# The first projection chain of a two-layer cross-attention kernel in two groups, and the last out-projections inside the last unit

## The reference

```
layer 0:  x = x + selfattention(LN(x))
          x = x + crossattention(LN(x), LN(context))        16 heads of 8 channels
          h = LN(x); x = h's residual x + top-2 of 8 experts (gelu MLP of width 512)
layer 1:  x = x + crossattention'(LN(x), context), its four weight matrices made ternary
each attention: softmax(q k^T / sqrt(8)) v, then out-projection with bias
```

## Time and profile before

| what | value |
|---|---|
| runs of the kernel before | 583.17, 574.94, 576.57 us |
| median | 576.57 us |
| the profiled execution | 574.07 us, of which the span of instructions is 572.3 us |
| PE, DVE, ACT, POOL busy | 514.1, 390.0, 334.4, 221.3 us |
| TensorE clock granted, mean of the span | 0.962 of full |

### The profile page before, as it was taken

The page is one execution under the profiler, slowest core; times in us unless marked ns, Lnnn a source line. Parts: engine busy times, 40 slices in busy tenths (PEclk is TensorE's granted clock), DMA queues, the critical chain, the costliest instruction groups (busy, mean ns, idle before and its releaser), DMA issues.

```text
span 572.3 us, 16262 instructions
## 1 busy us (share of the span) xinstructions
PE 514.1 (90%) x6648; PEld 386.4 (68%) x6648; DVE 390.0 (68%) x976; ACT 334.4 (58%) x527; POOL 221.3 (39%) x217
## 2 busy tenths in 40 slices
PE   3599748889999999999989999999998999999996
PEld 2588515466767767676767998877666676766774
DVE  5666378788887888787741434887867777786730
ACT  1166223557676777776576444376666667675573
POOL 3659744475777768423160200031404033140000
PEclk9799677899999999999999999999999999999998
DMA  5110552634354554555638401006354835535200
GB/s 160 48 55 3 143 122 50 169 89 132 95 139 112 143 145 101 137 120 143 182 73 223 141 2 31 2 1 154 72 150 113 201 92 140 144 85 121 56 4 9
DMA packets 37869, 58.69 MB, mean 103 GB/s; under 512 B 17956, under 2 KB 21404, under 8 KB 37796
## 3 DMA queue, kind: packets, MB, share of 16 engines
q1 hardware_dynamic: 37476, 57.60, 39.8%
q10 hardware_dynamic: 320, 0.06, 0.1%
HBM read 17.81 MB, written 0.23 MB: 32 GB/s over the span
## 4 chain that ended last, share of the span: by engine, by line
PE 68%; DVE 17%; POOL 4%; DMA 3%; issue 3%; ACT 2%; SPq 2%; DVEq 0%; ACTq 0%; POOLq 0%
PE PO L1386 14%; PE SM L1371 14%; DVE mxp L883 11%; PE ST L1343 10%; PE MI L1292 8%; PE ST L1564 4%; PE ST L1554 4%; PE MI L1282 3%; PE MI L1271 2%; POOL cxs L518 2%; PE MI L1318 2%; DMA xT<-in_ctxT 1%; ACT pts L671 1%; PE SM L1477 1%; SPq L393 1%
## 5 line engine op out<-in xcount | busy, mean ns | idle before, releaser
L883 DVE TENSOR_REDUCE mxp<-SM 112x1 f32<-112x500 f32 x374 | 241.0, 673 | 74.4 <-PE SM L1371 73.2
L671 ACT ACTIVATE pts<-ST 128x896 f32<-128x896 f32 x192 | 171.7, 913 | 31.3 <-PE ST L1343 30.8
L1371 PE MATMUL SM<-kst,qst 96*112 96x500 bf16 x374 | 142.2, 399 | 13.0 <-DVE mxp L883 9.0
L527 POOL TENSOR_TENSOR kr<-kf,ksplit 128x500 f32<-128x500 f32 x48 | 55.1, 1150 | 172.4 <-ACT ksplit L636 172.4
L1343 PEld LDWEIGHTS ST<-qst,kst 98*128 98x128 bf16 x1536 | 95.8, 100 | 29.5 <-issue 4.7
L1343 PE MATMUL ST<-qst,kst 98*128 98x112 bf16 x1536 | 106.9, 213 | 2.6 <-DMA qst<-mrow 2.6
L1386 PE MATMUL PO<-pts,vaug 125*32 125x112 f32 x3072 | 97.3, 263 | 2.3 <-ACT pts L671 1.9
L1371 PEld LDWEIGHTS SM<-kst,qst 96*112 96x112 bf16 x374 | 45.6, 129 | 61.5 <-DVE mxp L883 45.0
L1386 PEld LDWEIGHTS PO<-pts,vaug 125*32 125x32 f32 x3072 | 69.3, 109 | 14.8 <-ACT pts L671 5.7
L518 POOL TENSOR_SCALAR cxs<-cxs,cmv,crstd 125x128 f32<-125x128 f32 x84 | 67.4, 819 | 0.0
L532 POOL TENSOR_TENSOR ksplit<-kr,ksplit 128x500 bf16<-128x500 f32 x48 | 54.4, 1135 | 16.9 <-DVE ksplit L878 16.9
(11 more groups left out here) (156 smaller groups left out, 539.8 us busy)
## 6 DMA issues: line engine op xcount, KB each, us to landing
kst<-ksplit SPq DMA_DIRECT2D x192, 187.5 KB, 3.6
cxs<-in_ctx SPq DMA_DIRECT2D x8, 750.0 KB
xT<-in_ctxT SPq DMA_DIRECT2D x8, 750.0 KB, 6.5
qst<-qall SPq DMA_DIRECT2D x56, 21.0 KB, 1.9
watt<-in_watt SPq DMA_DIRECT2D x1, 768.0 KB, 5.5
cxs<-in_w1T SPq DMA_DIRECT2D x3, 256.0 KB, 5.7
cxs<-in_w2T SPq DMA_DIRECT2D x3, 256.0 KB, 6.3
pts<-in_w1T SPq DMA_DIRECT2D x3, 256.0 KB, 5.4
```

Source lines behind the costliest of these rows:

```text
L527: nc.gpsimd.tensor_tensor(kr[:, c], kf[:, c], ksplit[n.par][:, 0, c], ALU.subtract).then_inc(kr_done, 1)
L671: nc.scalar.activation(PT[:, k % PTB], ST[:, k % 2, :, 0:4 * PC], ACT.Exp, scale=SCALE).then_inc(exp_done, 1)
L883: nc.vector.tensor_reduce(mxp[:, j // 3, j % 3:j % 3 + 1], tile_bank(j, banks), AX.X, ALU.max).then_inc(sm_red, 1)
L1371: mm(tile_bank(j, banks), qst[n.par][0:SROWS, j // 3], kst[n.par][0:SROWS, j // 3, at:at + THIRD], start=True, stop=True).then_inc(sm_full, 1)
```

## The change

The four tiles' first chain becomes two groups (`PARTS`): tile 0 alone, and tiles 1 to 3.

- Tile 0's chain runs in steps 8 to 11 of self-attention, whose scores bank SM[0] is free by then: out-projection and statistics in step 8 (POOL's power ahead of the one for unit 2's context), normalise and transpose in 9, gain and query projection in 10, split in 11. Its six DMAs follow unit 0's restack; the load of unit 3's context moves behind them.
- After self-attention PE projects unit 1's keys and two thirds of unit 0's values, and the start tiles begin, 21 in place of 18. Both halves of `place_q` stand before them.
- The chain of tiles 1 to 3 stands among the start tiles: out-projection after tile 2 on PE, addition and statistics after tile 3 on DVE, and so on to the split after tiles 14 to 16. Statistics of unit 3's context stand at tile 12 and in steps 3 and 4 of the first window, which has 27 tiles in place of 30.
- POOL computes `token_rstd(2)` between `k_rest` and `k_third_part` of unit 1.
- In every out-projection the bias matmul comes first and the wait stands behind it.
- At the end: the out-projection of tiles 0 and 1 of layer 1 moves from window 5 to step 3 of window 7, tile 2's goes to its step 10, and only tile 3's is left for the end, with one store each.
- The second half of layer 1's query chain moves by a few steps, and its DMAs from SP's window 1 to window 2.

```diff
-START_TILES = 18
+START_TILES = 21
-FIRST_TILES = spread_tiles(TILES - START_TILES, (3, 3, 3, 3, 2, 2, 3, 3, 2, 2, 2, 2))
+FIRST_TILES = spread_tiles(TILES - START_TILES, (3, 3, 3, 3, 2, 2, 2, 2, 2, 2, 2, 1))
-LN5_AT, Q2_AT = (1, 3), (1, 9)
+LN5_AT, Q2_AT = (0, 10), (1, 10)
+START_OUT, START_ADD, START_NORM, START_LN, START_Q, START_SPLIT = 2, 3, 7, 9, 13, (14, 15, 16)
...
+PARTS = (range(0, 1), range(1, TT), range(0, HT), range(HT, TT), range(0, HT), range(HT, TT))
+OUT_PARTS = (range(0, 1), range(1, TT), range(0, HT), range(HT, TT), range(0, HT), range(HT, HT + 1), range(HT + 1, TT))
+OUT_MISC = (0, 2, 4, 5)
...
             load_ctx(Unit(0, None, 2))
-            load_ctx(Unit(0, None, 3))
             restack(u0, 0)
             restack(u0, 1)
             load_qall(0)
+            load_ctx(Unit(0, None, 3))
             place(u1, 0)
             restack(u1, 0)
+            load_qall(1)
...
                 if i == 8:
+                    token_rstd(1)
                     ctx_rstd(u0 + 2)
...
-            token_rstd(1)
+            k_parts(u1, None, lambda: token_rstd(2))
             ctx_normalise(u0 + 2, (2,))
-            k_parts(u1, None)
-            ctx_rstd(u0 + 3)
...
+                if i == 8:
+                    add_projection(0)
+                    token_stats(1)
+                if i == 9:
+                    token_normalise(1)
+                if i == 10:
+                    token_gain(1)
+                if i == 11:
+                    split_q(0)
...
             place_q(first, 0)
+            place_q(first, 1)
             for j in range(START_TILES):
                 reduce_tile(first, j, banks=4)
+                if j == START_ADD:
+                    add_projection(1)
+                    token_stats(2)
+                if j == START_NORM:
+                    token_normalise(2)
+                if j == START_LN:
+                    token_gain(2)
+                if j in START_SPLIT:
+                    split_q(1, (START_SPLIT.index(j),))
-                if j in (1, 4, 7):
-                    k_second_part(first + 1, j // 3)
+                if j in (1, 5, 12):
+                    k_second_part(first + 1, (1, 5, 12).index(j))
+                if j == TILES // 2:
+                    ctx_stats(u0 + 3, range(6))
...
-                    mm(tile, attnT[:, TP * t:TP * (t + 1)], watt[:, layer, 3], start=True, stop=False)
-                    last = mm(tile, ones_row[:], rows[0:1, D * layer:D * (layer + 1)], start=False, stop=True)
+                    mm(tile, ones_row[:], rows[0:1, D * layer:D * (layer + 1)], start=True, stop=False)
+                    if i == 0:
+                        pe.wait_ge(*done)
+                    last = mm(tile, attnT[:, TP * t:TP * (t + 1)], watt[:, layer, 3], start=False, stop=True)
...
-                    if n.s == 1 and (n.c, k) == OUT_AT:
-                        prev = project_out(3, (ont_evac, B + B // 2), prev)
+                    if n.s == 1 and (n.c, k) == (7, 3):
+                        prev = project_out(4, (ont_evac, B + B // 2), prev)
+                    if n.s == 1 and (n.c, k) == (7, 10):
+                        prev = project_out(5, (ont_evac, B + B - 2), prev)
...
             for j in range(START_TILES):
                 max_tile(u0, j, banks=4)
-                if j in (1, 4, 7):
-                    prev = project_v(u0, j // 3, prev)
-                if j in (10, 13, 16):
-                    prev = transpose_ctx(u0 + 2, (10, 13, 16).index(j), prev)
+                if j == 0:
+                    prev = project_v(u0, 2, prev)
+                if j == START_OUT:
+                    project_out(1, (sa_att, B))
+                if j == START_LN - 1:
+                    prev = transpose_tokens(2, prev)
+                if j == START_Q - 1:
+                    prev = project_q(1, prev)
+                if j in (10, 14, 17):
+                    prev = transpose_ctx(u0 + 2, (10, 14, 17).index(j), prev)
```

More of the change, by code:

```diff
@@ L437, in window @@
                     restack(nxt, 1)
+                if n.s == 1 and n.c == 2:
+                    load_qall(3)
                 if n.s == 0 and (n + 4).exists():
@@ L445, in window @@
                     load_xT(xT_unit)
-                if n.s == 1 and n.c == 1:
-                    load_qall(2)
                 if n.s == 0 and n.c in (3, 4):
@@ L474, in _ @@
             rows_out = out.rearrange("(t p) d -> p t d", p=TP)
-            for h in range(2):
-                sp.wait_ge(x_added, 4 + h)
-                sp.dma_start(rows_out[:, HT * h:HT * (h + 1)], xt[:, HT * h:HT * (h + 1)]).then_inc(stored, 16)
-            sp.wait_ge(stored, 32)
+            for n in range(4, 7):
+                sp.wait_ge(x_added, n + 1)
+                ts = OUT_PARTS[n]
+                sp.dma_start(rows_out[:, ts[0]:ts[-1] + 1], xt[:, ts[0]:ts[-1] + 1]).then_inc(stored, 16)
+            sp.wait_ge(stored, 48)
         @block.gpsimd
@@ L558, in window @@
                     k_parts(k_unit, None)
+                if n.first():
+                    ctx_rstd(n + 3)
                 if n.s == 0 and (n + 3).exists():
@@ L729, in evac_piece @@
                     evac_xT(n, (third,))
-                else:
+                if kind == "k":
                     evac_k(n, third)
@@ L824, in token_gain @@
                     dve.wait_ge(ld_vec, 16)
-                cols = slice(TP * token_tiles(n)[0], TP * (token_tiles(n)[-1] + 1))
-                src = SM[:, 0, 0:N] if n < 2 else MI[:, 0:HN]
+                cols = token_cols(token_tiles(n))
+                src = (SM[:, 0] if n < 2 else MI)[:, 0:cols.stop - cols.start]
                 nc.vector.tensor_scalar(hT[:, cols], src, ln_vec(X_LN[n], 0), ln_vec(X_LN[n], 1),
@@ L830, in split_q @@
             def split_q(n, parts=range(3)):
-                c = slice(0, N) if n == 0 else slice(HN * (n - 1), HN * n)
-                src, layer = (SM[:, 0, 0:N], 1) if n == 0 else (MI[:, 0:HN], 2)
+                c = token_cols(Q_TILES[n])
+                src, layer = (SM[:, 0] if n == 0 else MI)[:, 0:c.stop - c.start], n // 2 + 1
                 if 0 in parts:
@@ L1063, in window @@
                         copy_gates(0)
+                    if n.s == 1 and (n.c, k) == (0, 4):
+                        token_stats(6)
                     if n.s == 1 and (n.c, k) == (0, 9):
[L1065 removed]
+                        token_normalise(6)
                     if n.s == 1 and (n.c, k) == (0, 11):
[L1067 to L1069 removed]
+                        token_gain(6)
                     if n.s == 1 and (n.c, k) in SPLIT2_AT:
[L1071 to L1073 removed]
+                        split_q(3, (SPLIT2_AT.index((n.c, k)),))
+                    if n.s == 1 and (n.c, k) == (7, 5):
+                        add_projection(4)
+                    if n.s == 1 and (n.c, k) == (7, 11):
+                        add_projection(5)
+                    if n.first() and k == 3:
+                        ctx_stats(n + 3, range(6, NCH))
+                    if n.first() and k == 4:
+                        dve.wait_ge(cstat_ready, (n + 3).count(1, 1))
+                        ctx_aggregate(n + 3)
                     if ln_unit is not None:
@@ L1465, in piece @@
                     return transpose_ctx(n, third, prev)
-                return project_k(n, third, prev)
+                if kind == "k":
+                    return project_k(n, third, prev)
+                if kind == "out":
+                    pe.wait_ge(ld_rows, 48)
+                    pe.wait_ge(sa_sub, B)
+                    project_out(0, (sa_att, 2))
+                if kind == "ln":
+                    transpose_tokens(1, (x_added, 1))
+                if kind == "q":
+                    project_q(0, (hT_ready, 2))
+                return prev
             for i in range(SA_STEPS):
```

146 lines of the change are left out of this document (66 added, 80 removed).

## The result

The changed kernel takes 582.23 us in the median of 20 runs (577.62 to 590.4), the kernel before 577.96 us in 20 runs beside them (573.65 to 583.3). The ratio is 1.0077, 95% interval 1.0048 to 1.0105: slower by 0.8%, about 4.4 us (2.8 to 6.1), and so within 2%. I had forecast 577.5 us, in the range 572.5 to 583. The time is inside it, near its upper end, and the sign is right; but the three parts of the sum are all off: the start one way, the middle and the end the other.

A forecast was written before the change was run, and what follows sets the result against it. PE was taken to bound the whole span, DVE the start tiles. Start +3.4, middle 0 and end -1.2 gave +2.2 us on a base of 575.3: 577.5 us, range 572.5 to 583.

The forecast's parts named there:

- step 1: Self-attention: tile 0's addition and statistics on DVE delay unit 2's power and the restack by 1.8 us, bounds 0 to 3.
- step 2: Start: after restacks and `qall` transfers the first max tile comes at 81.5 instead of 86.14, a gain of 4.6 us.
- step 3: First tile to window 1: DVE's work, with unit 3's context and the chain of tiles 1 to 3, sums to 45.2 us.
- rival C: Start tiles: casts of keys and split slow down beside POOL; if two suffer, +4 us, 581.5 us; chance 0.05.
- step 4: First tile to window 1: DVE idles 7.0 us, 4.0 in the start tiles and 3.0 in the first window.
- step 5: Window 1 starts at 134.2 instead of 130.8, 3.4 us later, bounds 129.7 to 138.7.
- The middle: Layer 1's second query chain moves by some steps; nothing there waited before, so 0 us, bounds -0.5 to +0.5.
- The end: Last out-projections and store: end 2.0 us nearer, window 5 gains 1.6, window 7 loses 2.4; net 1.2 us gained.
- A: Start: the added DVE work slides into its idle time, if idle stays below 4.8 us; 573.5 us, chance 0.28.
- B: First window: unit 1's restack comes late and PE stalls 3 us for `kst` in step 1; 580.5 us, chance 0.15.
- D: Start: `qall` issues or self-attention slip 3 us more, first tile at 84.5 or later; +5, 580.5 us; chance 0.05.
- The signs: Expected trace marks: `place_q` waiting, DVE over 85% busy in start tiles, scores at 104 to 107, store about 2 us nearer.

The follow-up runs named there:

- e1: The changed kernel with layer 1's second query chain and the end put back as before, so only the start changed: 588.02 us, ratio 1.0175 to the kernel before.
- e5: The changed kernel with the chain of tiles 1 to 3 ahead of the first tile, casts of K and values placed as before: 568.83 us, ratio 0.9836.
- e7: The changed kernel with both the chain of tiles 1 to 3 and unit 3's context statistics ahead of the first tile: 567.51 us, ratio 0.9817.
- e10: The changed kernel with unit 1's second cast of K after tile 2 in place of tile 5: 580.34 us, ratio 1.0067.
- e9: The changed kernel with nine unread matmuls on PE, six ahead of the first tile, three ahead of the tokens' transposes: 581.8 us, ratio 1.0079.
- e3: The kernel before with only layer 1's second query chain and its transfers moved: 573.33 us, ratio 0.9925.
- e2: The kernel before with only the end changed (last out-projections and bias matmuls first): 576.24 us, ratio 0.9960.
- e4: The kernel before with layer 1's second query chain and the end changed, the start left as it was: 571.91 us, ratio 0.9898.

## Why the prediction was right and wrong

*Self-attention (step 1), +1.8 us: right in size.* In e1, whose start is that of the changed kernel, SP began the restack at 64.89, where I had 65.4. The four kernels with the same self-attention whose early stretch at the lower clock ended near 30 us (e1, e5, e7, e10) have the last `attnT` at 67.8 to 68.4, 2.5 to 3.1 us behind the 65.31 of before. In the profiled execution of the changed kernel that stretch ran from 19.1 to 36.2 us in place of 20.6 to 30.8, in instructions that the change does not touch, and the last `attnT` came at 69.85. These 2 us are chance of that one execution, but they can't be taken off the +10.9: e1 and e10 had the earlier `attnT` and still reached window 1 at 141.56 and 141.72, because their start tiles ran at the lower clock throughout and took 30.6 and 30.1 us in place of 27.8. The timed difference (4.4) is smaller than that of the spans (5.5), but its interval, to 6.1, holds it.

*The first tile (step 2), 81.5: right.* In e1 it came at 81.26 and in the changed kernel at 84.20, later by about what self-attention was late. SP's order is as forecast, 10 us of restacks and then `qall`:

```profile
67.75 10.05 SPq L434 DMA_DIRECT2D kst<-ksplit  x12
77.85 4.61 SPq L415 DMA_DIRECT2D qall<-qsplit  x6
```

*DVE's work (step 3), 45.2 us: short by 2.6.* From the end of `place_q` at 84.52 to window 1 it was 47.8. Summed by operation in both traces, overlaps counted once, 5.1 us were added for the chain of tiles 1 to 3 (forecast 5.7), 3.8 for unit 3's context (3.6), 0.7 for one maximum more that falls before window 1 and 2.2 for the casts of K, and 0.4 went with `place_q` (0.5). The casts are rival C, to which I gave a chance of 0.05: the cast at 93.55 took 2.33 us. In the sum itself it stood at nothing.

*DVE's idle time (step 4), 7.0 us: short by 2.4.* It was 9.4, 5.75 in the start tiles (forecast 4.0) and 3.6 in the first window (3.0). The gaps that I had worked out are there (1.44 and 1.44, the second with the clock at its upper level; in e1, at the lower level, the second was 3.42). The failed step is the sum of the gaps: I had worked out only how long PE's pieces take and put PE's waits for DVE in front of them at nothing, and they measured 4.20 and 2.45 us on PE and 1.8 us of DVE's idle time behind the first. In the two traces whose start tiles ran at the lower clock throughout (e1 and e10) DVE's idle time to window 1 was 11.8 us, in the changed kernel 9.4, in e9 8.3: the idle time goes with the clock, by 2.4 us between e1 and the changed kernel, which have the same start.

*Window 1 (step 5), 134.2.* It was 84.5 + 47.8 + 9.4 = 141.7 where I had 82.0 + 45.2 + 7.0. The miss of 7.5 is 2.5 for the first tile, 2.6 for the work and 2.4 for the idle time. The bounds I gave, up to 138.7, did not hold it: they varied idle time and first tile, but not the work.

*The middle, 0: wrong, -3.7.* The sentence "Nothing in this stretch waits for them before" failed: PE waited 2.65 us in window 1 of layer 1 (see e3).

*The end, -1.2: too small, -2.3.* The steps are those that I named, and the timeline shows them:

```profile
574.43 0.27 PEld L1272 LDWEIGHTS PO<-rows,ones_row 1*112 1x112 f32 x2
574.60 0.31 ACT L707 ACTIVATE attnT<-ST,vec 128x56 f32<-128x56 f32 x1 [1.90 <-PE ST L1371]
574.96 0.27 PEld L1275 LDWEIGHTS PO<-watt,attnT 128*112 128x112 f32 x2 [0.26 <-ACT attnT L707]
574.96 0.47 PE L1275 MATMUL PO<-watt,attnT 128*112 128x128 f32 x2
575.47 0.29 DVE L954 TENSOR_TENSOR xt<-xt,PO 112x128 f32<-112x128 f32 x1 [1.45 <-PE PO L1275]
```

From the last `attnT` to the end of the span it is 2.87 us in place of 5.67: -2.8, not -2.0. Behind the last `attnT` there is one pair, 0.47 us at the upper clock, where four took 2.8 at the lower: 2.3 saved, where I had 2.1. The 0.2 that I took off for too little room was not needed, since the bias pair is over at 574.90 and the last `attnT` at 574.91. The addition is 0.13 shorter, and from the store's issue to the end of the span it is 1.99 us in place of 2.35, which I had at nothing. Window 5 gained the 1.55 that I had said, and the last window up to that point grew by 2.0 (18.12 to 20.11), not by 2.4. The net of these is -2.35 in the profile, and e2's ratio gives -2.3.

*The rivals.* A (0.28) did not happen: 9.4 us idle, where it wanted less than 4.8. B's waits were not seen: no wait of PE for `kst` in step 1, since scores started at 112, far behind B's 106; the restack itself started at 105.47, later than B's 102.5. C happened at its place, with one cast of the four. D's first tile, 84.5 or later, nearly came (84.20), but with self-attention's clock and not by what the change does.

*The signs.* `place_q` waited for `qall` in front of the first tile, and the last store was issued 2.4 us nearer to the last `attnT`, as forecast. The signs behind the first tile did not come: DVE was busy for 79% of the start tiles and not over 85, with two gaps of 1.44 us and not one of 2 to 4 before the fourth maximum, the first scores came at 112 and not at 104 to 107, and window 1 was 10.9 us later and not two to five.

So the forecast was close because a start mis-sized by +7.5 stood against a middle and an end mis-sized by -3.7 and -1.1. That is luck. Of the 4.7 us by which the time itself is off, 2.7 are the base: I had put it at 575.3, and the kernel before ran at 577.96. The result's sign came for the reason given (DVE's load moved from a stretch that waits into one in which it is the slower engine): e5, the change with that load left in the wait, is 1.6% faster than before, not 0.8% slower. Middle and end are 1.0% of this (e4); the start costs 1.75% in e1 and gains about 0.6% in e5. As e5 also moves casts of K and values, this shows the start's order as a whole, not the chain by itself.

## What to carry to other kernels

When a first piece of a chain is pulled forward, what is left of the chain should take the wait that becomes free, and not stand among work behind it. Put into a busy stretch, it costs its own time and also the other engine's pieces and each handover between in-order engines: here 5.5 us of idle time beside 8.0 of work, of which the chain itself is 5.1. Before an instruction is called free in its new place, list the waits of the engine there in the trace of before, and look for waits of the old place too: the largest gain of this change, 4.3 us, was for the most part a few removed waits of 0.5 to 0.8 us that only a query of that window shows.

## What the hardware did that I had not expected

**A cast that starts just behind one of POOL's subtractions ends just behind it.** In rival C I wrote that of 48 casts only the one at 56.6 had been slow. That was a misreading of a median (the page itself gives these casts a mean of 729 ns, beside the median of 411): single rows of the same trace show thirteen more of 1.33 or 1.34 us, each started within 0.1 us behind a POOL subtraction of 1.14 and ended 0.3 us behind its end, such as:

```profile
141.75 1.14 POOL L532 TENSOR_TENSOR ksplit<-kr,ksplit 128x500 bf16<-128x500 f32 x1
141.84 1.33 DVE L878 CAST ksplit<-kr 128x500 bf16<-128x500 f32 x1 [0.17 <-POOL kr L527]
```

The changed kernel has the same pattern, at 93.55 beside two of POOL's operations back to back:

```profile
93.38 1.13 POOL L555 TENSOR_TENSOR ksplit<-kr,ksplit 128x500 bf16<-128x500 f32 x1
94.47 1.13 POOL L550 TENSOR_TENSOR kr<-kf,ksplit 128x500 f32<-128x500 f32 x1
```

The cast ended at 95.88, behind the second. The tile maxima, which read PSUM, keep their 0.65 to 0.68 us beside POOL's work. The operations that stretched (the casts of K, `xn` in e10 at 2.06 and in e5 at 1.26, `mparts`) read and write SBUF. Not all that do so stretch: twelve statistics of the context (L879) beside POOL's subtractions in the changed kernel took 0.27 to 0.29 us each, as elsewhere. Nor does each operation of POOL do it: in the kernel before, the cast at 48.11 took 0.40 us beside POOL's `TENSOR_SCALAR` (L518, from 47.74), and the one at 293.10, beside a POOL operation of 2.90 (L539, from 293.03), 1.38. The Trainium skill, "Advanced Engine Details and Errata", section "VectorE Performance Modes", says that DVE's second SBUF port is shared with GpSimd, and that GpSimd's instructions and DVE's two-port instructions block each other. The rows beside the subtractions agree, where the prediction had set the rule aside, and those at 48.11 and 293.10 do not as it stands; which mode an operation ran in, no run here shows. Beside a subtraction the price is not a share of the operation's time but about the rest of POOL's, whatever the length of DVE's own: 0.17 us became 1.15.

**The clock falls earlier or later in the same code.** Up to step 7 of self-attention the kernels do the same, and yet the first stretch at the lower level ended at 30.2 to 38.0 us in the traces of these kernels, having lasted 10.2 to 20.5 us, and the last `attnT` moved with it. In e4, whose self-attention is that of before, it ran from 17.9 to 31.6 us and the last `attnT` came 2.0 us later than in the profile of before. Window 6 of layer 1 shows the same late in the program: in seven of the fourteen traces the clock fell there for 3.4 to 10.2 us, and the window took 24.9 to 27.3 us in place of 23.5. What sets it in a single execution stays open. So a term of 2 us that is read from one profiled execution can be chance.
